# Value products of an attention slot in one piece, with both pairs' probabilities kept

## The reference, cut to what matters

```
x: 32 x 64 x 512, context: 32 x 64 x 512, 32 query heads, 8 key/value heads of 128
h = layernorm(x);  q = h @ Wq;  k = ctx @ Wk;  v = ctx @ Wv;  q, k = rope(q), rope(k)
attn = softmax(where(mask == 0, -1e9, q k^T / sqrt(128)))
x = x + (attn v) @ Wo
r = softmax(layernorm(x) @ gate_w^T)
x = x + (layernorm(x) * (r @ in_scale)) @ sign(weight)^T * (r @ out_scale) + bias
```

## Time and profile before

| what | value |
|---|---|
| median of 3 runs | 1192.29 us (1191.25 to 1193.23) |
| the profiled execution's own time | 1192.27 us |
| its span, first to last instruction | 1189.5 us |
| PE busy | 1156.4 us, 97% |
| PE weight loads busy (beside the matmuls) | 949.7 us, 80% |
| DVE busy | 809.9 us, 68% |
| ACT busy | 552.3 us, 46% |
| POOL busy | 712.0 us, 60% |
| mean granted clock of PE | 0.992 |

### The profile page before, as it was taken

The page is one execution under the profiler, slowest core; times in us unless marked ns, Lnnn a source line. Parts: engine busy times, 40 slices in busy tenths (PEclk is TensorE's granted clock), DMA queues, the critical chain, the costliest instruction groups (busy, mean ns, idle before and its releaser), DMA issues.

```text
span 1189.5 us, 23750 instructions
## 1 busy us (share of the span) xinstructions
PE 1156.4 (97%) x7636; PEld 949.7 (80%) x7636; DVE 809.9 (68%) x1367; ACT 552.3 (46%) x1768; POOL 712.0 (60%) x593
## 2 busy tenths in 40 slices
PE   5699999999999999999999999999999999999997
PEld 4588888888888888888888888888888888888875
DVE  6767676667776766777766667667677666666764
ACT  3444445444543544444544544544544444535442
POOL 5666655555775656765555766655667555766525
PEclk9999999999999999999999999999999999999997
DMA  8234333223422322333322322323332222322200
GB/s 227 79 111 120 93 94 89 79 81 100 121 90 63 88 79 88 120 99 97 107 67 71 106 79 87 97 83 105 89 98 81 64 72 68 97 75 87 78 2 35
DMA packets 136923, 106.02 MB, mean 89 GB/s; under 512 B 12776, under 2 KB 111080, under 8 KB 136864
## 3 DMA queue, kind: packets, MB, share of 16 engines
q1 hardware_dynamic: 131488, 94.78, 27.5%
q10 hardware_dynamic: 4608, 8.39, 2.1%
q0 software_dynamic: 768, 2.10, 0.6%
HBM read 101.05 MB, written 4.19 MB: 88 GB/s over the span
## 4 chain that ended last, share of the span: by engine, by line
PE 94%; DVE 3%; POOL 1%; issue 1%; ACT 1%; DMA 0%; POOLq 0%; DVEq 0%; ACTq 0%
PE chunk L1045 25%; PE chunk L1046 24%; PE chunk L1047 24%; PE o_ps L1118 5%; PE sc_ps L1093 3%; PE tr_ps L1093 2%; PE aux L1034 2%; PE o_ps L1034 1%; PE tr_ps L1034 1%; PE sc_ps L1034 1%; PE aux L1195 1%; PE aux L1196 1%; PE aux L1169 1%; PE aux L1181 0%; ACT probs L547 0%
## 5 line engine op out<-in xcount | busy, mean ns | idle before, releaser
L408 POOL TENSOR_TENSOR w_lo<-raw,w_hi 128x512 fp32r<-128x512 f32 x192 | 247.0, 1298 | 384.6 <-ACT w_hi L511 384.4
L801 DVE TENSOR_TENSOR swp<-chunk,sinT 64x512 f32<-64x512 f32 x320 | 220.3, 689 | 98.8 <-PE chunk L1047 94.4
L1045 PE MATMUL chunk<-xT_hi,w_hi 128*128 128x512 f32 (+1 forms) x512 | 210.0, 410 | 2.0 <-POOL w_lo L408 1.8
L1046 PE MATMUL chunk<-xT_lo,w_hi 128*128 128x512 f32 (+1 forms) x512 | 201.6, 394 | 0.0
L1047 PE MATMUL chunk<-xT_hi,w_lo 128*128 128x512 f32 (+1 forms) x512 | 200.6, 392 | 0.0
L1045 PE MATMUL chunk<-wo_hi,oT_hi 128*128 128x512 f32 x496 | 196.7, 397 | 0.1
L1047 PE MATMUL chunk<-wo_hi,oT_lo 128*128 128x512 f32 x496 | 193.7, 391 | 0.0
L1046 PE MATMUL chunk<-wo_lo,oT_hi 128*128 128x512 f32 x496 | 193.2, 389 | 0.0
L415 POOL TENSOR_TENSOR qT<-qT,swp 128x512 f32<-128x512 f32 x128 | 166.1, 1298 | 41.2 <-DVE qT L803 39.2
L547 ACT ACTIVATE probs<-scores,neg_max 128x64 f32<-128x64 f32 x512 | 170.4, 335 | 28.5 <-DVE neg_max L758 28.5
L743 DVE TENSOR_TENSOR acc<-chunk,acc 128x512 f32 (+1 forms) x128 | 88.2, 689 | 139.3 <-PE chunk L1047 139.1
(11 more groups left out here) (281 smaller groups left out, 1934.7 us busy)
## 6 DMA issues: line engine op xcount, KB each, us to landing
raw<-in_L_xattn_Wo SPq DMA_DIRECT2D x132, 256.0 KB, 2.6
raw<-in_L_xattn_Wq SPq DMA_DIRECT2D x128, 256.0 KB, 2.7
raw<-in_L_xattn_Wk SPq DMA_DIRECT2D x32, 256.0 KB
raw<-in_L_xattn_Wv SPq DMA_DIRECT2D x32, 256.0 KB
acc<-in_x ACTq DMA_DIRECT2D x16, 256.0 KB, 2.9
c_tile<-in_ctx SPq DMA_DIRECT2D x12, 256.0 KB, 3.1
x_tile<-in_x SPq DMA_DIRECT2D x12, 256.0 KB, 3.4
result<-y ACTq DMA_DIRECT2D x12, 256.0 KB, 2.1
```

The lines of the kernel that those rows point to most:

```text
L408: nc.gpsimd.tensor_tensor(lo, raw[:, n % RING, :], hi.bitcast(F32), ALU.subtract).then_inc(wsplit_lo, 1)
L801: last = nc.vector.tensor_tensor(swp[to, k, :], bank[of, :], sinT[to, here], ALU.mult)
L1045: nc.tensor.matmul(bank, a_hi, b_hi, start=i == 0, stop=False)
L1046: nc.tensor.matmul(bank, a_hi, b_lo, start=False, stop=False)
```

## The change

The value products of a slot are issued in one piece, `values(s, 0)` and at once `values(s, 1)`, between `project(s, 1)` and `project(s, 2)`; before, `values(s, 1)` stood between `project(s, 3)` and `project(s, 4)`. For this:

- the transposed probabilities get a buffer for each duo, and duo 1's results go to the two banks in which the scores and the transposed probabilities stood (`duo_ps`); `values(s, 1)` no longer waits for `out_lo` of duo 0
- ACT makes the high part of duo 1's probabilities at once behind duo 0's, and `out_hi` of pairs 2 and 3 stands before `split_hi(s, 6)`
- DVE makes both low parts before `rotate(s, 0)`, and `out_lo` of pairs 2 and 3 stands before `rotate(s, 3)` in place of behind it
- `f_tile` and `fT` become other names for `x_tile` and `c_tile`, which pays for the second probability buffer. SP therefore has two more waits, in slots 6 and 7 of quarters 1 and 2, and the context tile's load moves behind the first two weight chunks of its slot. POOL's order is as it was.

```diff
-        pT_hi, pT_lo = (sb(n, [P, 2, 2 * P], F32R) for n in ("pT_hi", "pT_lo"))
+        pT_hi, pT_lo = (sb(n, [P, DUOS, 2, 2 * P], F32R) for n in ("pT_hi", "pT_lo"))
...
-        c_tile, x_tile, f_tile, fT = (sb(n, [P, E]) for n in ("c_tile", "x_tile", "f_tile", "fT"))
+        x_tile, c_tile = sb("x_tile", [P, E]), sb("c_tile", [P, E])
+        f_tile, fT = x_tile, c_tile
...
-        sc_ps, tr_ps, aux = (stack.enter_context(nc.psum_tensor(n, [P, 512], F32)) for n in ("sc_ps", "tr_ps", "aux"))
-        o_both = stack.enter_context(nc.psum_tensor("o_ps", [P, 2, 512], F32))
+        aux = stack.enter_context(nc.psum_tensor("aux", [P, 512], F32))
+        duo_both, o_both = (stack.enter_context(nc.psum_tensor(n, [P, 2, 512], F32)) for n in ("duo_ps", "o_ps"))
         o_ps = [o_both[:, i, :] for i in range(2)]
+        sc_ps, tr_ps = (duo_both[:, i, :] for i in range(2))
...
+        OUTPUTS = [o_both, duo_both]
...
-        x_first = [x_tile, f_tile, fT, y]
+        x_first = [x_tile[:, :], swp[:, 0, :], swp[:, 1, :], y[:, :]]
...
+                self.past_ffn = intake and not residual and not isinstance(g, int)
...
         @block.sync
-            def load_tile(t):
+            def load_x(s, t):
+                sp.wait_ge(x_tr, t)
+                if s.past_ffn:
+                    sp.wait_ge(fn_tr, s.q * PAIRS)
+                sp.dma_start(x_tile[:, :], row_of(x_t, t)).then_inc(x_in, 16)
+            def load_c(s, t):
                 sp.wait_ge(c_tr, t)
+                if s.past_ffn:
+                    sp.wait_ge(xs_l, s.q * PAIRS)
                 sp.dma_start(c_tile[:, :], row_of(ctx_t, t)).then_inc(c_in, 16)
-                sp.wait_ge(x_tr, t)
-                sp.dma_start(x_tile[:, :], row_of(x_t, t)).then_inc(x_in, 16)
             def load_weights(s):
                 for n in range(CH):
+                    if s.intake and n == 2:
+                        load_c(s, jobs_of(s)[0][0])
...
         ACT, slot(s)
                     pT_hi_split(s, 0)
+                    pT_hi_split(s, 1)
...
                 if s.attn:
-                    pT_hi_split(s, 1)
                     out_hi(s, 0)
                     out_hi(s, 1)
...
                     split_hi(s, 5)
+                if s.attn:
+                    out_hi(s, 2)
+                    out_hi(s, 3)
+                if s.proj:
                     split_hi(s, 6)
                     split_hi(s, 7)
...
                     xs_split(f[0], in_slot)
-                if s.attn:
-                    out_hi(s, 2)
-                    out_hi(s, 3)
-                if s.ffn:
                     out_scales(f[0], in_slot)
...
         PE, values(s, d)
-                else:
-                    pe.wait_ge(o_lo, 2 * n)
...
-                            last = nc.tensor.matmul(o_both[:, b, bass.ts(i, HG * S)], v[keys, 2 * d + i, :], probs_of[keys, i, :],
+                            last = nc.tensor.matmul(OUTPUTS[d][:, b, bass.ts(i, HG * S)], v[keys, 2 * d + i, :], probs_of[keys, d, i, :],
                                                     start=k == 0, stop=k == 2)
...
         PE, slot(s)
                     values(s, 0)
+                    values(s, 1)
...
                     project(s, 3)
-                if s.attn:
-                    values(s, 1)
```

More of the change, by code:

```diff
@@ L290, in heads_of_o @@
         def heads_of_o(p):
-            return o_both[:, :, bass.ts(p % 2, HG * S)].rearrange("p b (h s) -> p b h s", h=HG)
+            return OUTPUTS[p // 2][:, :, bass.ts(p % 2, HG * S)].rearrange("p b (h s) -> p b h s", h=HG)
         def rope_out(j):
@@ L358, in slot @@
                 if s.intake:
-                    load_tile(jobs_of(s)[0][0])
+                    load_x(s, jobs_of(s)[0][0])
                 if s.proj:
@@ L544, in exp_duo @@
                 if not s.first_attn:
-                    act.wait_ge(probs_tr, n - 1)
+                    act.wait_ge(probs_tr, n - DUOS + 1)
                 for k in part:
@@ L555, in pT_hi_split @@
                 act.wait_ge(probs_tr, n + 1)
-                if not (s.first_attn and d == 0):
-                    act.wait_ge(pv_done, n)
-                copy(flat2(pT_hi), DUO_BANK[d][:, :]).then_inc(pT_h, 1)
+                if not s.first_attn:
+                    act.wait_ge(pv_done, n - DUOS + 1)
+                copy(flat(pT_hi[:, d, :, :]), DUO_BANK[d][:, :]).then_inc(pT_h, 1)
             def out_hi(s, p):
@@ L776, in pT_lo_split @@
                 dve.wait_ge(pT_h, (s.U - 1) * DUOS + d + 1)
-                lo_of(flat2(pT_lo), DUO_BANK[d][:, :], flat2(pT_hi)).then_inc(pT_l, 1)
+                lo_of(flat(pT_lo[:, d, :, :]), DUO_BANK[d][:, :], flat(pT_hi[:, d, :, :])).then_inc(pT_l, 1)
             def out_lo(s, p):
@@ L916, in slot @@
                     ffn_constants()
+                if s.attn:
+                    pT_lo_split(s, 0)
+                    pT_lo_split(s, 1)
+                if s.ffn:
+                    router_max(f[0], in_slot)
                 if s.proj:
                     rotate(s, 0)
-                if s.ffn:
-                    router_max(f[0], in_slot)
-                if s.attn:
-                    pT_lo_split(s, 0)
                 if s.intake:
@@ L928, in slot @@
                     rotate(s, 1)
-                if s.attn:
-                    pT_lo_split(s, 1)
                 if s.ffn:
@@ L941, in slot @@
                     scales_lo()
-                if s.proj:
-                    rotate(s, 3)
                 if s.attn:
@@ L946, in slot @@
                     out_lo(s, 3)
+                if s.proj:
+                    rotate(s, 3)
                 if s.ffn:
```

## The result

The changed kernel takes 1221.6 us (median of 4 runs, 1221.34 to 1221.98) where the kernel before takes 1191.9: 2.5% slower, ratio 1.0248 with a 95% interval of 1.0230 to 1.0266. The forecast was 1212.5 with a range of 1200 to 1222. The direction, the place and the price in the slots without FFN came out as forecast; the FFN slots did not.

What follows compares the result with a forecast made beforehand. PE bounds the kernel, with a chain project 3, DVE, POOL, next slot right behind it. 19 x 1.28 = +24.3 and 12 x -0.34 = -4.1 make +20.2 on 1192.27: 1212.5 us, range 1200 to 1222.

Steps and rivals of the forecast that it cites:

- PE's gain from joining the blocks: Value products on PE: one entry and exit saved, 0.40 us in slots without FFN, 0.34 in FFN slots.
- The first rival: PE's time alone counts: the chain doesn't reach PE, all slots keep their gain, 11.7 us, 1180.6 us; chance 0.10.
- The chain in slots without FFN: Project 3, `out_lo`, `rotate(s, 3)`, POOL's `rope_sum(s, 3)` and chunks 8 and 9, next slot: +1.28 us in 19 slots.
- POOL's readiness: Before `rope_sum(s, 3)`: POOL free at 9.3 us from the first value product, needed at 10.34; covered with 1.0.
- the values' new wait: Start of the value products: both duos' low parts needed, ready at 582.9 against 584.76; cover 1.8 us, cost nothing.
- the shared tiles at nothing: `f_tile` and `fT` in `x_tile` and `c_tile`: shared tiles change no duration; SP's waits and context load taken as 0.
- FFN slots: Twelve slots, 0.34 us shorter each, -4.1 together; 1.76 us of slack at the end was to cover POOL's delay.
- 0.6 us of cover: DVE's queue behind the low parts ends at 588.9, before `rotate(s, 2)` at 589.54; else that rotate is late.
- The clock: Rival: PE's clock falls if two waits a slot lower it 19 times, +33 us, 1246; chance 0.07.
- the forecast's own terms: Range from PE's answer, start after a wait, FFN slots and four loads: 1208 to 1219 us.
- rivals of which none named this cause: PE alone 1180.6 (0.10), hidden `out_lo` 1201.3 (0.08), clock 1246 (0.07), new wait in the slot's first half 1228 (0.05).
- answer, FFN and one late load: Upper ends: PE's answer to POOL +2.1 us, FFN slots' gain only 0.17 each +2.0, one SP load +3.

Runs made afterwards that it cites:

- experiment 7: Changed kernel with `out_lo` of pairs 2 and 3 behind `rotate(s, 3)`, routing ahead of `rotate(s, 0)`, POOL's chunks 8 and 9 ahead of `rope_sum(s, 3)`: 1180.2 us.
- Experiments 1 and 2: Changed kernel with, first, `out_lo` of pairs 2 and 3 behind `rotate(s, 3)`: 1211.3 us; second, POOL's chunks 8 and 9 ahead of `rope_sum(s, 3)`: 1201.6 us.

## Why the prediction was right, and where it was not

- *PE's gain from joining the blocks* (0.40 and 0.34 us a slot): right in kind, and a little too small. It is real, but in the changed kernel no slot's length shows it; experiment 7 does, with 0.47 to 0.5 and 0.38 us. Most of the rest lies in the matmuls behind a block, whose steps the forecast rounded to 0.23: they are (588.32 - 586.00) / 10 = 0.232 us in the projection behind a block and (591.04 - 588.32) / 12 = 0.227 in the next one, about 0.06 us over a projection. The first rival (1180.6) named a state that exists, only not with this order.
- *The chain in slots without FFN* (+1.28 us a slot): right, +1.27, each step within 0.05 us. That is for a typical slot; the mean of the 19 is 1.23. Experiments 1 and 2 cut the chain at two places and got what each place was said to cost (0.60 for 0.59; 1.10 for 1.07).
- *POOL's readiness, the values' new wait, the shared tiles at nothing*: right. The values start in the same place, POOL reaches `rope_sum(s, 3)` with 0.84 us of idle time, and the memory part alone measures 1.0004.
- *FFN slots* (12 x -0.34 = -4.1): wrong, +6.7. These 10.8 us are more than the whole error of the forecast (9.1 by the medians); the 19 other slots gave back 1.0 of them. The step that failed is in two parts. First, DVE's queue between the low parts and `rotate(s, 2)` was worked out for the intake slot, with 0.6 us of cover, and carried over. For the FFN slot that left out the routing, and with it the chance that DVE comes to the routing while POOL is splitting; it took 1.32 us in place of 0.24, and `rotate(s, 2)` started 0.6 us late. Second, the FFN slot was checked only at its end, where chunk 9 was to be 0.23 us ahead of PE. PE's own waits for the FFN steps inside the slot were put at nothing without a reason, and there the time was lost. At the end POOL was done at 722.37 + 2.55 = 724.92, still 0.84 us ahead of the next slot at 725.76.
- *The clock*: right; the granted clock read 0.992 in both kernels, with some 1.2 us of idle PE a slot.

The median lay inside the range (1200 to 1222) by luck: the forecast's own terms gave 1208 to 1219, and the upper end had been taken out towards rivals of which none named this cause. That 1219 doesn't follow from the terms as written either: answer, FFN and one late load make +7.1, while four loads at +3 each would have reached 1228.6. The runs put the loads at nothing (1.0004 for the memory part alone). The forecast did say what a failure would look like: "If FFN slots get longer too, it is wrong in their slack."

## What to carry to other kernels

When a stretch of the bound engine gets shorter, list what the others still have to do in it: here PE's way from project 3 to the next slot shrank to 5.7 us, while the chain through DVE and POOL behind it needed 6.7. The same order on POOL cost nothing before and 20 us after, so an order that a measurement has shown to be free has to be looked at again after each change beside it. And an instruction that will run at another time, even one that keeps its place in its queue, has to be costed beside what runs on the other engines then.

## What the runs showed of the hardware

Some DVE instructions are held until POOL's running instruction ends, here one that is itself short: 235 ns with POOL idle, 1231 to 1327 ns when it fell 0.00 to 0.10 us behind the start of a POOL `tensor_tensor` of 128x512 (1.3 us), for `tensor_scalar` with its tensor input from SBUF and for `tensor_tensor` with two inputs from SBUF alike; 244 ns with the tensor input in PSUM. The row shows it as a long busy time, not as idle time, so the lists of waits don't have it; the same form with two different means does. DVE's `tensor_tensor` with one input in PSUM and one in SBUF, such as `oT_lo<-duo_ps,oT_hi`, ran beside POOL at their usual 0.68 us each (form means of 681 to 683 ns here and 682 in the kernel before).

The Trainium skill says this in "SBUF — State Buffer", section Terms: DVE and GpSimd arbitrate for one pair of ports, locked for a whole instruction, and the loser is blocked. The Trainium skill's "GPSIMD Engine Reference", section Specifications, adds that this holds for DVE's instructions in a two-port mode or with two inputs in SBUF. The traces agree: held with two inputs in SBUF (1327 ns), held as `tensor_scalar` from SBUF (1319 ns), not held from PSUM (244 ns). In which mode the `tensor_scalar` ran no trace shows.

The other: a block of pairs over 64 partitions between matmuls over 128 costs 0.40 us at its edges beside its inner pace, and joining two blocks made slots without FFN 0.47 to 0.5 us shorter and FFN slots 0.38 (experiment 7). The change of banks in the middle of the joined block costs nothing: its steps stay at 0.12 us. The pairs differ from the projections' matmuls in their columns too (256 in place of 512), and no run tells which of the two the edges pay for.
